# Constant products ahead of the query transposes, of three attention tiles and of the last scores

## The reference, cut to what matters

```python
h = _layernorm(x) * (1 + ca) + sa
q, k, v = h @ Wq, h @ Wk, h @ Wv            # 16 heads of 8, rotated, elu + 1
beta = clip(sigmoid(h @ Wbeta + bbeta), 0.001, 0.999)
def step(carry, inp):
    M, Z = carry
    q_t, k_t, v_t, b_t = inp
    M = M * b_t[:, :, None, None] + (k_t[:, :, None] * v_t[:, None, :])[:, None]
    Z = Z * b_t[:, :, None] + k_t[:, None, :]
    num = einsum('bd,bcde->be', q_t, M)
    den = einsum('bd,bcd->b', q_t, Z) + EPS
    return (M, Z), num / den[:, None]
x = x + ga * layernorm(h + scan(step) @ Wo + bo)
h = _layernorm(x) * (1 + cb) + sb
x = x + gb * (top-2 experts of 8, each w2 @ silu(w1 @ h), with a capacity) + ...
```

## Time and profile before

| | |
|---|---|
| median of 3 runs | 296.11 us |
| lowest and highest of them | 294.85 and 299.49 us |
| the profiled execution, its own time | 293.68 us |
| its span, first to last instruction | 291.9 us |
| outside the span | 1.8 us |
| mean granted TensorE clock | 0.886 |
| TensorE, VectorE, ScalarE, GpSimd busy | 251.4, 209.2, 121.2, 90.0 us |
| TensorE idle until "issue", L1612 | 6.5 us, 7 times |

### The profile page before, as it was taken

One profiled execution on the slowest core, in us unless ns is written; L12 is line 12 of the kernel. 1 busy time (PEld: TensorE's weight loads), 2 busy tenths in 40 slices (PEclk: granted clock), 3 DMA queues, 4 the chain that ended last, 5 costly groups with the idle time before them and its releaser, 6 DMA issues. The chain is left out here.

```text
span 291.9 us, 11345 instructions
## 1 busy us (share of the span) xinstructions
PE 251.4 (86%) x4731; PEld 188.4 (65%) x4731; DVE 209.2 (72%) x828; ACT 121.2 (42%) x274; POOL 90.0 (31%) x102
## 2 busy tenths in 40 slices
PE   7997898799977999899887889988999999999900
PEld 3665657676566855678555564436898889888800
DVE  5697989849699597986778568837557655756563
ACT  4598258652668444753322122203233432343200
POOL 0030014000023406052134216740544464546630
PEclk9999579779998799955999596999999999999965
DMA  6980000030700103000021001122424433331566
GB/s 178 338 311 4 3 2 6 4 146 4 291 4 4 30 3 112 13 4 12 22 80 46 21 6 57 45 80 86 129 55 130 147 96 108 121 100 36 172 214 227
DMA packets 18197, 25.19 MB, mean 86 GB/s; under 512 B 2679, under 2 KB 11400, under 8 KB 18146
## 3 DMA queue, kind: packets, MB, share of 16 engines
q1 hardware_dynamic: 14434, 19.18, 20.5%
q0 software_dynamic: 2368, 4.24, 4.5%
q10 hardware_dynamic: 1344, 1.05, 1.1%
HBM read 12.84 MB, written 12.15 MB: 86 GB/s over the span
## 5 line engine op out<-in xcount | busy, mean ns | idle before, releaser
L948 ACT ACTIVATE arena<-ps 128x385 f32<-128x385 f32 (+1 forms) x64 | 27.6, 439 | 62.3 <-PE ps L1876 61.6
L685 POOL DMA_INDIRECT pair_out<-arena,meta x40 | 39.2, 981 | 45.0 <-DVE arena L1407 19.2
L631 POOL DMA_INDIRECT dispatched<-row,idx x32 | 32.5, 1014 | 60.2 <-PE ps L1619 27.6
L1893 PE MATMUL ps<-w2t,arena 128*128 128x128 f32 x320 | 40.4, 278 | 0.0
L1893 PEld LDWEIGHTS ps<-w2t,arena 128*128 128x128 f32 x320 | 39.3, 191 | 0.9
L1512 PE MATMUL ps<-later_b,ident_b 128*128 128x512 bf16 x141 | 38.1, 409 | 0.0
L1876 PE MATMUL ps<-arena,w1t 128*128 128x256 f32 (+1 forms) x128 | 37.6, 434 | 0.2 <-issue 0.2
L1407 DVE SCALAR_TENSOR_TENSOR arena<-ps,meta,arena 128x128 f32<-128x128 f32 x40 | 14.0, 351 | 26.4 <-PE ps L1893 15.4
L654 POOL TENSOR_TENSOR arena<-arena,ex 128x256 f32<-128x256 f32 x16 | 10.7, 695 | 68.2 <-DVE arena L1029 50.2
L1612 PE MATMUL ps<-v,wts 32*32 32x9 f32 x2048 | 24.0, 180 | 8.8 <-issue 6.5
L1612 PEld LDWEIGHTS ps<-v,wts 32*32 32x32 f32 x2048 | 22.0, 117 | 13.5 <-issue 13.1
(11 more groups left out here) (182 smaller groups left out, 446.3 us busy)
## 6 DMA issues: line engine op xcount, KB each, us to landing
dispatched<-fill SPq DMA_DIRECT2D x12, 260.0 KB, 4.2
pair_out<-zero SPq DMA_DIRECT2D x6, 512.0 KB, 3.4
arena<-dispatched SPq DMA_DIRECT2D x8, 325.0 KB, 3.0
w1t<-in_w SPq DMA_DIRECT2D x8, 256.0 KB, 2.7
w2t<-in_w SPq DMA_DIRECT2D x8, 256.0 KB, 3.1
arena<-pair_out SPq DMA_DIRECT2D x4, 512.0 KB, 5.1
const<-in_constants SPq DMA_DIRECT2D x1, 803.5 KB, 6.5
X<-in_x SPq DMA_DIRECT2D x1, 768.0 KB, 7.6
```

The lines of the kernel that those rows point to most:

```text
L631: pool.indirect_dma_start(disp_d, bass.IndirectOffsetOnAxis(ap=idx[:, p.g, t, k:k + 1], axis=0), row[:, p.g, t, k, :], None, bounds_check= ...
L685: pool.indirect_dma_start(pair_d, bass.IndirectOffsetOnAxis(ap=meta[:, u, a, 0:1].bitcast(U32), axis=0), orow[:, u, a, :], None, bounds_ch ...
L948: a_.activation(hid[:, u, f, c0:c0 + cn], ps[:, k % 4, 0:cn], ACT.Silu).then_inc(hid_done[u].sem, 1)
L1893: m = mm(row_bank(u, a)[:, 0:P], hid[:, u, f, 1 + a * P:1 + (a + 1) * P], w2t[:, u, f, :], start=(f == 0), stop=(f == FT - 1))
```

## The change

It adds 36 constant products and three explicit waits, and removes and moves nothing else. In each of the three bodies with `more`: 3 ahead of `query_T(n)`, 3 ahead of `attention(g, 2)` and 2 ahead of `attention(g, 3)`. In the last body: 5 ahead of `scores(g, 3)` and 6 in place of 4 ahead of `attention(g, 3)`. At the start: 5 ahead of `attention(0, 0)`. Each wait that is written ahead of products stands in the old code in the step behind them or, ahead of `query_T`, one step later (in `scores(g, 3)`).

```diff
@@ pe_body
                 adds(g, 3)
+                pe.wait_ge(w_done.sem, w_done.now(g, 3))
+                keep_streaming(ps[:, 0, :], 3 if more else 5)
                 if more:
                     query_T(n)
                 scores(g, 3)
                 if more:
                     query_factors_T(n)
+                    pe.wait_ge(y_done.sem, y_done.now(g, 2))
+                    keep_streaming(T6, 3)
                     attention(g, 2)
                     key_T(n)
+                    pe.wait_ge(w_done.sem, w_done.now(g))
+                    keep_streaming(ps[:, 0, :], 2)
                     attention(g, 3)
@@ the last body
                     pe.wait_ge(w_done.sem, w_done.now(g))
-                    keep_streaming(ps[:, 0, :], 4)
+                    keep_streaming(ps[:, 0, :], 6)
                     attention(g, 3)
@@ ahead of the bodies
             adds(0, 1)
+            keep_streaming(T6, 5)
             attention(0, 0)
```

## The result

The changed kernel takes 304.93 us (median of 4 runs, 302.86 to 310.18), the kernel before beside it 295.48 us (4 runs, 293.42 to 299.49). The ratio is 1.032, with a 95% interval of 1.024 to 1.040: slower by over 2%. The forecast was 299.0 us in a range of 290.0 to 303.5, so the direction was right and the size was not: 1% where 3.2% was measured, and the time lies above the range.

What follows compares the result with a forecast made beforehand. Bound: the chain through VectorE and TensorE to GpSimd's last write, with TensorE stopping at pages of 256 instructions. The terms sum to +4.4 on 293.68 us (298.1), plus 0.9 towards the median: 299.0 us, range 290.0 to 303.5.

Steps and rivals of the forecast that it cites:

- Start 0: Start: 5 products ahead of an attention that stopped for a page cost nothing; 0, bounds -0.8 and +0.2 us.
- Body 0, -1.0: Body 0: added products fill waits and lift the clock, the moved edge in attention 3 is harmless; -1.0 us.
- Body 1, +1.5: Body 1: edges move into the adds and attention 3's closing products; +1.5 us, between +1.1 and +2.8.
- Body 2, +1.5: Body 2: edge moves into the end of attention 1, so query transposes start later; +1.5 us, bounds 0 and +1.9.
- Last body, adds and scores, +0.9: Last body: an edge moves from the scores into the adds, with 5 unhidden products ahead of the scores; +0.9 us.
- Last body, attention 3, +1.5: Last body: a second edge falls into attention 3's 16 closing matmuls, reached at 172.1, released at 174.3; +1.5 us.
- Behind it, nothing: After the last body: the delay reaches the end in full through GpSimd's writes, with nothing added.
- From the profiled execution to the median, +0.9: Whole kernel: the median lay 2.4 us above the profiled execution; 0.9 of it was added.
- the lines L1639 and L1619: New TensorE "issue" waits of some 2 us: L1639 (adds), L1619 (attention 3), in body 1 and the last.
- stops bring the clock down too: Rival: work behind the 2.2 us stops runs at 1.2 GHz, slower by over 2%, 303.4 us; chance 0.23.
- The clock wins: Rival: page edges cost no more than before and only the clock changes, 286.7 us; chance 0.15.
- Nothing moves: Rival: shorter slow stretches (-4) and longer stops (+4) cancel, 296.1 us; chance 0.17.

Runs made afterwards that it cites:

- e1: The changed kernel with the 10 wide products of its start issued as 106 narrow ones, later page edges 64 instructions later in the work: 291.46 us, ratio 0.985.
- e8: The changed kernel with the start in 90 narrow products of 57 columns, page edges 96 instructions later in the work: 291.97 us, ratio 0.995.
- e2: The kernel before with the 10 wide products of its start issued as 34 of 128 columns, 48 instructions more: 302.87 us, ratio 1.025.
- e6: The changed kernel with the start in 122 narrow products of 42 columns, page edges 32 instructions later in the work: 295.04 us, ratio 0.989.
- e5: The changed kernel with e1's start and all 36 added products 16 columns wide, as in e3: 296.75 us, ratio 1.011.
- e3: The changed kernel with each of the 36 added products 16 columns wide in place of 512, same page edges: 302.86 us, ratio 1.018.
- e4: The changed kernel with only the 3 products ahead of the query transposes and the 5 ahead of the last scores 16 columns wide: 303.90 us, ratio 1.025.
- e7: e1 with 64 instructions more at the end of body 2, so only the last body has the changed kernel's edges: 294.01 us, ratio 1.003.
- e10: The changed kernel a third time, unchanged, one run: 305.94 us.
- e9: The changed kernel once more, unchanged, one run: 301.68 us.

## Why the prediction was wrong

The mechanism was right: the edges that were counted, in the adds and in the closing products of body 1 and of the last body, fell there and stopped TensorE. What failed is one size that was picked between its bounds, and a kind of stop for which the sum has no term.

**Point by point**, predicted and measured (differences of the stations above):

- Start 0: right. The stop of the earlier trace rows is gone, and the second projection began at 37.48, as VectorE's logits allow.
- Body 0, -1.0: measured -0.26. The edge in attention 3, called harmless, still stopped it (0.63 us at 55.93, before 0.39), and behind it came the low-clock stretch from 58.1, on the transposes and the projection.
- Body 1, +1.5: measured +3.07, the first large miss. Both edges fell where they were counted, in the adds and in the 16 closing products, and the pages came as said: 86.37 for 86.3, 97.69 for 97.7. queries_T was 0.86 late for the predicted 0.8 (the text says once "starts near 88" for a start at 89.2). That delay was gone again by the closing products, at 95.30 against 95.12. What went wrong is the choice between the bounds +1.1 and +2.8: own_norm stood at 103.03, +2.81 against before, the upper one, since the work between the stop and own_norm ran at 1.2 GHz. The other 0.26 is body 0's gain, which was lost again.
- Body 2, +1.5: measured +0.90, by another way than told, so that this term came near by luck. The query transposes were 3.63 later than before (128.23 for 124.60) and queries_T only 2.56, so this part gave back 0.25 of the 2.81 brought along. The loss is an edge in attention 3 that the prediction had not followed (1.84 us at 138.57).
- Last body, adds and scores, +0.9: measured +1.54 (5.25 less 3.71). The stop in the adds was 0.44 and not 1.8 us: the page ahead of it took 2.7 us to use up, part of it at 1.2 GHz, and the next was there 3.1 us after its entry; the five products behind it cost 2.31, their upper price; and 1.4 us of stops within a page came on top.
- Last body, attention 3, +1.5: measured +2.61, but the edge itself cost the 1.5. The closing products took 2.3 us more than before (177.98 to 180.71, before 172.42 to 172.83), and the old stop inside attention 3 and a wait ahead of it gave back 0.8. The other 1.1 us came in attention 2, which took 2.31 us for 1.17 because of the two stops within a page at 173.42 and 174.12. The clock was down behind the stop, but it was before as well.
- Behind it, nothing: measured +0.42, GpSimd's writes of the last group standing wider apart.
- From the profiled execution to the median, +0.9: measured +2.1 (304.93 for 302.86), and another 0.9 around the span that the sum hadn't. 293.68 and 8.28, 0.9 and 2.1 make the 304.9.

**The failing steps** are thus these. In body 1 the term "+1.5" counted on a clock that would be mostly up behind the stop of 2.2 us; it was down, and the term is 3.1. In the last body the two terms "+0.9" and "+1.5" have nothing for stops that are not at a page edge; the changed kernel stood still for 2.1 us by them there, and attention 2 alone took 1.1 us longer. Their cause stays open. Body 0's gain (0.7 too large) and the steps from the span to the median (2.1 us too small together) are sizes too. Counted at what bodies 1 and 3 measured, the two "+1.5" make 5.7 in place of 3.0.

**The sums.** The terms' lower bound adds up to -1.4, not -1.5; nothing hangs on it.

**Of the signs to look for**, the lines L1639 and L1619 were right. "Issue" grew from 7.8 to 13.6 for a predicted 8 to 13, but the stops at page edges grew to 10.7 only, so the match is in part luck. own_norm of body 0 was not 1 us earlier but 0.26. The pace was wrong as a rule: most pages that stopped TensorE were entered some 3.5 us after the one before (3.46 us from 94.23 to 97.69), but the page of the last adds after 3.1 and that at the end of body 2's attention 1 after 2.5 us (124.46 to 126.96), below the 3.4 named as a refutation. The trace of before has such a one too: the stop that ended at 89.87 came 3.1 us after that page was entered, at 86.80 by the count. The low-clock sum went lower (27.3 for 38), and the time rose all the same.

**Of the rivals**, "stops bring the clock down too" had nearly the time, 303.4, with the wrong condition: it asked for some 50 us of slow stretches. Its mechanism needs only 3.4 us of them, behind each stop. "The clock wins" is what e1 and e8 show once the edges are away, though not at its 286.7. "Nothing moves" fell with the interval.

**Which part caused what.** Shown: most of the loss hangs on where the edges fall (e1 and e8 against the changed kernel, e2 against before, body 2 against body 1 inside e6), and the products' own time isn't the cause (e1). Shown by a narrow margin: the products are a gain at harmless edges (e5 against e1 and e8). Not shown by a run of its own: how the loss at an edge divides between the stop and the low clock behind it, which is read from one body of e8 (2.26 and 1.5 us), and how the loss divides between bodies 1 and 2. The stops within a page, 2.9 us in the changed kernel, are a part that isn't told apart either: e3 and e4 have the same edges and none of these stops, and took 1 to 2 us less by the median of their own runs. Open: why stops within a page appear, and the half of the last body's loss that e7 did not repeat.

## What to carry to other kernels

When an engine's program is long and has bursts of very short instructions, count its instructions (a weight load, a matmul and a semaphore instruction are one each), mark every 256th from the stops that the trace shows, and look which edges lie in a burst that someone waits for; a change that adds instructions anywhere moves all later edges and can cost more there than it gains. Before such a change is judged, try it at two or three shifts made by splitting work that waits anyway: the same 36 products were 1.032, 0.985, 0.989 and 0.995 of the time before. And a sum of low-clock time is no measure of the cost: read where the stretches lie against the engine that waits.

## What was not expected of the hardware

- 48 instructions at the start, with fewer columns to stream, made a kernel 2.5% slower (e2).
- Pages have no fixed pace like the 3.66 us of the earlier trace rows: TensorE stopped 2.5 us after the entry of the page before (e2, at 89.69, and the changed kernel, at 126.96) and as late as 4.7 us after it (e2, at 157.18). In e10 it went on into the next page 1.3 us after the entry without a stop (127.86 to 129.13). Steadier is the time from the fetch: in all twelve traces a stop at an edge ended 2.2 to 3.0 us after the last 16 KB packet on the instruction queue had begun (in the changed kernel 97.69 after 95.28). That packet began mostly some 1.1 us after a page was entered, in e10's case 1.3 us ahead of it (126.57). What sets that moment is open.
- TensorE stopped inside a page too, in all three executions of the changed kernel and not in those of before and e1 to e8: in the scores of body 2 (0.44 and 0.32, 1.13, 1.14 us), in those of the last body and in its attention 2. GpSimd was issuing indirect writes (L631) in or just ahead of them, but in the last scores of e3 it did so too, without such a stop. The cause is open.
- The last edge's stop vanished in e9 when the attention ahead of it ran at 1.2 GHz, and own_norm's second half came no earlier for it.
